# The second half of a batch's value products moved into the next round, and its inverses behind the next statistics

## The chip, the cores and the metric

The kernel runs on one core of a Trainium2 chip. The metric is the device time of one execution in microseconds (us). In the profile PE is the matrix engine (TensorE; PEld are its weight loads), DVE the vector engine, ACT the scalar engine, POOL the GpSimd engine, and SP the engine that issues most DMAs. L939 is line 939 of the kernel before.

## The reference

One transformer block over a batch of 32, each with 165 tokens (a class token, 36 image patches, 128 text tokens) of width 256. The change touches the attention alone.

```python
h = tok_ref(x)                               # 1 + 36 embedded patches per batch
h = concatenate([h, txt], axis=1)            # (32, 165, 256)
h = h + attn(layernorm(h))                   # 16 heads of 16, causal mask, every 4th key dropped
h = h + ffn(layernorm(h))                    # router, 8 experts, the top 660 tokens of each

def attn(x):
    q, k, v = heads(x @ Wq + bq), heads(x @ Wk + bk), heads(x @ Wv + bv)
    att = einsum('bhtd,bhsd->bhts', q, k) / sqrt(16)
    att = softmax(where(mask == 0, -inf, att), axis=-1)
    return (einsum('bhts,bhsd->bhtd', att, v)) @ Wp + bp
```

## The kernel before

Each engine has its own program, written out by hand in a fixed order, and the programs meet at semaphores. The attention part is a software pipeline of rounds, `for b in ROUNDS`: round b works at several batches at once. In round b the matrix engine makes the queries, keys and values of batch b+2, the masked scores by rows of batch b+1 (`row_scores`, from which the vector engine takes the row maxima), and the scores by keys of batch b (`key_scores`), their exponentials being the probabilities. Batches go in pairs n = b // 2, u = b % 2: an even round also projects the pair before and adds the result to the residual, an odd round also transposes and routes the pair before that.

What the change touches:

- `mix_values(b, c)` on the matrix engine (L939): the value products of heads 8c to 8c+7 of batch b, and beside them the row sums of the probabilities by products with ones, into bank 2+c. It is made of four groups (V, ones, V, ones) of four products, each 32 columns of weights wide, side by side in the array. It waits for `causal_done`: GpSimd has put zeros where a key is later than the query (`zero_future`, L535, once for each quarter of the heads). Half c = 1 needs the last two of the four quarters.
- `heads_out(b, c)` on the vector engine: waits for `pv_done`, takes the inverse of the row sums (L1309) and multiplies the products by it (L1313), into `yT`.
- `queries(b + 2)` (L862) stands at the head of a round on the matrix engine; in a round after an odd one `route` (L965, ends the round before) stands ahead of it, and `copy_logits` (L1319) takes its result.
- `ln1_stats_of` (even rounds) and `ln2_stats_of` (odd rounds) on the vector engine: `bn_stats` (L1246) and `bn_aggr` (L1250), ahead of the round's row maxima.
- `row_max(m, i)`, i = 0 to 4 (L1298), with `low_q` and `low_k` (L1277) between. `row_scores(m, i)` (L898 for the mask, L901 for the products) alternates between banks 4 and 5: number i waits until the maxima of number i-2 are taken. `row_scores(m, 4)` (the form 65*65 of L898) so waits for `row_max(m, 2)`.
- SP packs the queries and keys (`pack`, L364 and L368) once `low_q` is done (`q_ready`), and behind that, in its own order, the maxima (`pack_max`, L373), which the next round's first `key_scores` needs (`m_packed`).

Of the kernel before, what the change touches and what calls it, by code (L numbers as in the profile page):

```python
# [15 lines left out]
B, CH, IMG, PATCH = 32, 3, 96, 16  # L16
# [110 lines left out]
def build(nc, xT, wl, h0, addrows, clsrows, minus, watt, vecs, rowv, w1, w2, const_f, const_b, out):  # L127
    ctx = ExitStack()
    with ctx:  # L129
# [135 lines left out]
        def bank(i):  # L265
            return ps_all[:, i, :]
# [57 lines left out]
        def apart(eng):  # L324

            eng.sem_inc(passed[eng], 1)
# [506 lines left out]
        def _(pe):  # L833
# [22 lines left out]
            def queries(n, free):  # L856
                u, h = n % 2, n // 2 % 2
                pe.wait_ge(xnT_ready, 2 * (n // 2) + 2)
                pe.wait_ge(*free)
                for c in range(KD):  # L860
                    for k in range(KD):
                        mm = pe.matmul(bank(6)[:, c * TE:(c + 1) * TE], W_q[:, k, c * 128:(c + 1) * 128],  # L862
                                       xnT[:, h, k, u * T:u * T + TE], start=(k == 0), stop=(k == KD - 1))
                mm.then_inc(q_done, 1)
# [63 lines left out]
            def mix_values(b, c):  # L928
                pe.wait_ge(causal_done, 4 * b + 2 * c + 2)
                if c == 0:  # L930
                    pe.wait_ge(v_ready, b + 1)
                if b >= 1:
                    pe.wait_ge(yT_ready, 2 * b + c - 1)
                for w in range(2):
                    for part in range(2):
                        for j in range(4):
                            dst = bank(2 + c)[32 * j:32 * j + 32, part * T:(part + 1) * T]
                            lhs = v_rows(b % 3, w, 4 * c + j)[0:S] if part == 0 else ones_eo[0:S, w, :]
                            mm = pe.matmul(dst, lhs, PT[0:S, 2 * c + w, j, :], start=(w == 0 and part == 0),  # L939
                                           stop=(w == 1), skip_group_check=True)  # L940
                mm.then_inc(pv_done, 1)
# [27 lines left out]
            def query_bank(b):  # L969
                n, u = divmod(b, 2)  # L970
                if b == -2:
                    return xnT_ready, 2
                if u == 1:
                    return (resid_ready, RT * (n - 1) + 2) if n >= 1 else (v_ready, b + 2)
                return (xn2T_ready, 2 * (n - 2) + 2) if n >= 2 else (xnT_ready, 2 * (n + 1) + 2)
# [46 lines left out]
            def round_of(b):  # L1022
                n, u = divmod(b, 2)
                has_q, has_r, has_s = b + 2 < B, b + 1 < B, b < B
                has_t1, has_p, m = n + 2 < NPAIR, 0 <= n - 1 < NPAIR, b + 1
                if has_q:
                    queries(b + 2, query_bank(b))
                if has_s:
                    key_scores(b, 0)
                if has_r:  # L1030
                    row_scores(m, 0, (max_ready, 5 * m))
                if has_q:
                    keys(b + 2, key_bank(b))
                if has_r:
                    row_scores(m, 1, (mT_ready, m))
                if has_s:
                    key_scores(b, 1)
                if has_r:
                    row_scores(m, 2, (max_ready, 5 * m + 1))
                if has_q:  # L1040
                    values(b + 2)
                if has_r:
                    row_scores(m, 3, (max_ready, 5 * m + 2))
                if has_r:
                    row_scores(m, 4, (max_ready, 5 * m + 3))
                if has_s:
                    key_scores(b, 2)
                if b == B:
                    project(n - 1, 0, (exp_done, 4 * B))
                    project(n - 1, 1, (exp_done, 4 * B))  # L1050
                    project(n - 1, 2, (max_ready, 5 * B))
                    route(n - 2)
                    return
                if u == 0 and has_p:
                    project(n - 1, 0, (k_ready, b + 3) if has_q else (logit_ready, n - 1))
                if u == 1 and has_t1:
                    transposes1(n + 2, 0, (k_ready, b + 3))
                if has_r:
                    max_transposes(m)
                if u == 0 and has_p:  # L1060
                    project(n - 1, 1, (v_ready, b + 3) if has_q else (xn2T_ready, 2 * (n - 2) + 2))
                if u == 1 and has_t1:
                    transposes1(n + 2, 1, (v_ready, b + 3))
                if has_s:
                    key_scores(b, 3)
                if u == 0 and has_p:
                    project(n - 1, 2, (resid_ready, RT * (n - 1) + 1))
                if b == B - 1:
                    mix_values(b, 0)
                    mix_values(b, 1)  # L1070
                if u == 1 and has_p:
                    for c in range(KD):
                        transposes2(n - 1, c, (xnT_ready, 2 * (n + 2) + c + 1) if has_t1 else
                                    ((k_ready, v_ready)[c], b + 3) if has_q else
                                    (resid_ready, RT * (n - 1) + 3 - c) if has_s else
                                    ((logit_ready, n - 1), (xn2T_ready, 2 * (n - 1)))[c])
                if has_s and b != B - 1:
                    mix_values(b, 0)
                    mix_values(b, 1)
                if u == 1 and has_p and b != B - 1:  # L1080
                    route(n - 1)

# [148 lines left out]
        def _(dve):  # L1231
# [29 lines left out]
            def ln2_stats_of(p):  # L1261
                dve.wait_ge(resid_ready, RT * p + RT)
                apart(dve)
                if p >= 1:
                    dve.wait_ge(shift2_ready, p)
                stats(p, st2, mv2, ln2_chain, ln2_stats)
# [56 lines left out]
            def round_of(b):  # L1323
                n, u = divmod(b, 2)
                has_q, has_r, has_s, has_p = -2 <= b < B - 2, -1 <= b < B - 1, 0 <= b < B, 0 <= n - 1 < NPAIR
                if b == -4:
                    embedded(1)
                if b == -2:
                    low_q(0)
                    low_k(0)  # L1330
                if u == 0 and n + 2 < NPAIR:
                    ln1_stats_of(n + 2)
                if u == 1 and has_p:
                    ln2_stats_of(n - 1)
                if b == B + 1:
                    copy_logits(n - 2)
                if b == -4:
                    for g in (2, 3, 4, 5):
                        embedded(g)
                if b == -3:  # L1340
                    dve.wait_ge(vec_in, 16)
                    for k in range(KD):
                        ins = dve.tensor_copy(bvB[:, k, :], bvT[:, k:k + 1].to_broadcast([128, A]))
                    ins.then_inc(bvB_ready, 1)
                    embedded(6)
                if b == -1:
                    for g in (7, 8):
                        embedded(g)
                    low_q(1)
                    low_k(1)  # L1350
                    embedded(9)
                    dve.wait_ge(bpe_done, 1)
                    dve.wait_ge(row_in, 16)
                    dve.tensor_tensor(bpe[0:A, :], bank(5)[0:A, 0:D], bp_s[0:A, :], ALU.add).then_inc(bpe_ready, 1)
                    embedded(10)
                if has_r:
                    row_max(b + 1, 0)
                if has_q and b >= 0:
                    low_q(b + 2)
                if has_r:  # L1360
                    row_max(b + 1, 1)
                if has_q and b >= 0:
                    low_k(b + 2)
                if has_r:
                    row_max(b + 1, 2)
                if has_r:
                    row_max(b + 1, 3)
                if has_r:
                    row_max(b + 1, 4)
                    copy_mT(b + 1)  # L1370
                if u == 0 and has_p:
                    for r in range(RT):
                        residual(n - 1, r)
                if has_s:
                    heads_out(b, 0)
                    heads_out(b, 1)
                if u == 1 and has_p and b != B - 1:
                    copy_logits(n - 1)

            embedded(0)  # L1380
            for b in ROUNDS:
                round_of(b)
# [350 lines left out]
```

## Time and profile before

| | |
|---|---|
| median of 3 runs | 832.5 us (829.48 to 835.09) |
| the profiled execution's own time | 832.7 us |
| its span in the trace | 831.0 us |
| PE busy | 739.2 us, 89% of the span |
| DVE, ACT, POOL busy | 68%, 48%, 46% |
| granted clock of TensorE, mean | 0.938 |
| attention rounds in the trace | about 50 to 455 us |

How to read it: a row of the timeline gives the start, the duration and the engine of a run of like instructions, and in brackets the time that the engine sat idle before it and what ended that. The rounds repeat: from round 3 on, two rounds take 25.5 us, and rows of one pair of rounds stand for the others. Rows below are of rounds 12 (even, from 204.12 us on the matrix engine) and 13 (from 216.34 us).

### The profile page before, as it was taken

Reading aid. Unit: us, or ns where it says so; the run is one execution under the profiler, and the core shown is the slowest. Engines: PE = TensorE matmul, PEld = TensorE weight load, DVE = VectorE, ACT = ScalarE, POOL = GpSimd, SP = SyncE. Lnnn points to the kernel's source line nnn. Section 1 sums busy time; section 2 is a strip of 40 time slices with the busy share of each in tenths; the row PEclk is TensorE's granted clock in tenths of the full one; section 3 lists DMA queues with packets and bytes.
Section 4 is the critical chain, followed back from the end, with each engine's and each line's share of the span. In section 5 each row is a group of like instructions: output and inputs, shape, how many; then the busy total and the mean of one; then the engine's idle time right before and its main releaser. Section 6 shows DMA issues by size and latency. Waiting matters only on the chain. (4 is left out here: it accounts for less than half of the span.)

```text
span 831.0 us, 18782 instructions
## 1 busy us (share of the span) xinstructions
PE 739.2 (89%) x6840; PEld 670.2 (81%) x6840; DVE 566.7 (68%) x1343; ACT 397.2 (48%) x858; POOL 384.1 (46%) x534
## 2 busy tenths in 40 slices
PE   6989999999999999999997412499999999999994
PEld 4878888888888888888875311399999999999994
DVE  1357778677686776776765377857788787787461
ACT  0334464454544554545543264045737558376470
POOL 4243464554544645546434342304735637356334
PEclk9999999999999999999998655569999999999998
DMA  9765766866747756568560522102345343443122
GB/s 311 202 100 93 112 111 110 141 109 113 108 94 113 117 93 88 106 100 122 97 101 20 185 77 95 33 1 84 59 127 148 42 135 59 124 100 40 33 29 33
DMA packets 80584, 82.38 MB, mean 99 GB/s; under 512 B 35705, under 2 KB 73575, under 8 KB 80236
## 3 DMA queue, kind: packets, MB, share of 16 engines
q1 hardware_dynamic: 66988, 64.96, 39.4%
q0 software_dynamic: 11840, 11.12, 8.3%
q10 hardware_dynamic: 1664, 5.09, 2.0%
q8 instruction: 55, 0.90, 0.5%
q14 instruction: 37, 0.30, 0.1%
HBM read 34.59 MB, written 16.22 MB: 61 GB/s over the span
## 5 line engine op out<-in xcount | busy, mean ns | idle before, releaser
L631 POOL DMA_INDIRECT out<-r_arena x48 | 81.3, 1695 | 116.3 <-DVE r_arena L1594 104.4
L535 POOL TENSOR_SCALAR_AFFINE_SELECT r_arena<-r_arena 126x660 f32<-126x660 f32 x128 | 97.0, 768 | 51.6 <-ACT r_arena L695 51.3
L695 ACT ACTIVATE r_arena<-ps_all 126x660 f32<-126x660 f32 x128 | 92.2, 720 | 57.5 <-PE ps_all L924 56.2
L1298 DVE TENSOR_REDUCE mx<-ps_all 128x4 f32<-128x504 f32 (+1 forms) x160 | 104.8, 668 | 15.8 <-PE ps_all L901 14.5
L1309 DVE RECIPROCAL r_arena<-ps_all 128x165 f32<-128x165 f32 x64 | 76.1, 1189 | 57.3 <-PE ps_all L939 57.3
L1616 DVE TENSOR_TENSOR hT_lo<-r_arena,hT_hi 128x330 fp32r<-128x330 f32 x128 | 63.3, 501 | 40.7 <-ACT r_arena L803 40.7
L901 PE MATMUL ps_all<-Kp,Qp 96*65 96x56 f32 (+1 forms) x512 | 90.6, 293 | 0.0
L618 POOL DMA_INDIRECT xe<-xn_rows,r_arena x48 | 60.3, 1255 | 62.4 <-issue 35.7
L924 PE MATMUL ps_all<-Qp,Kp 98*126 98x166 f32 x512 | 84.6, 288 | 4.5 <-ACT r_arena L695 2.9
L801 ACT ACTIVATE hT_hi<-ps_all,vec_s 128x330 fp32r<-128x330 f32 x128 | 68.9, 538 | 38.2 <-PE ps_all L1166 37.3
L1166 PE MATMUL ps_all<-xeT_hi,W_hi 128*128 128x330 f32 x256 | 83.5, 326 | 1.1 <-DVE xeT_lo L1608 1.1
L1166 PE MATMUL ps_all<-xeT_lo,W_hi 128*128 128x330 f32 x256 | 82.6, 323 | 0.0
L1166 PE MATMUL ps_all<-xeT_hi,W_lo 128*128 128x330 f32 x256 | 82.2, 321 | 0.0
L1186 PE MATMUL ps_all<-hT_hi,W_hi 128*128 128x330 f32 x256 | 81.6, 319 | 0.0
L1186 PE MATMUL ps_all<-hT_hi,W_lo 128*128 128x330 f32 x256 | 80.7, 315 | 0.0
L673 ACT ACTIVATE q_hi<-ps_all,vec_s 128x166 fp32r<-128x166 f32 x64 | 22.0, 395 | 122.2 <-PE ps_all L862 122.2
L1186 PE MATMUL ps_all<-hT_lo,W_hi 128*128 128x330 f32 x256 | 80.3, 314 | 0.0
L924 PEld LDWEIGHTS ps_all<-Qp,Kp 98*126 98x126 f32 x512 | 69.0, 190 | 10.1 <-ACT r_arena L695 6.5
L901 PEld LDWEIGHTS ps_all<-Kp,Qp 96*65 96x65 f32 (+1 forms) x512 | 66.8, 166 | 5.6
L803 ACT ACTIVATE r_arena<-ps_all,vec_s 128x330 f32<-128x330 f32 x128 | 67.9, 530 | 0.0
L939 PE MATMUL ps_all<-r_arena,V 126*32 126x165 f32 x1024 | 61.6, 313 | 1.1 <-POOL r_arena L535 1.0
L939 PE MATMUL ps_all<-r_arena,cf 126*32 126x165 f32 x1024 | 60.5, 309 | 0.0
(182 smaller groups left out, 1699.5 us busy)
## 6 DMA issues: line engine op xcount, KB each, us to landing
H<-w SPq DMA_DIRECT2D x16, 1024.0 KB, 5.8
Qp<-q_hi SPq DMA_DIRECT2D x64, 166.0 KB, 3.9
Kp<-k_hi SPq DMA_DIRECT2D x128, 63.0 KB, 4.0
Qp<-q_lo SPq DMA_DIRECT2D x32, 166.0 KB, 4.6
out<-H SPq DMA_DIRECT2D x16, 330.0 KB
xn_rows<-r_arena SPq DMA_DIRECT2D x16, 330.0 KB
Kp<-k_lo SPq DMA_DIRECT2D x64, 63.0 KB, 4.0
H<-h SPq DMA_DIRECT2D x11, 336.0 KB, 3.9
```

Source lines behind the costliest of these rows:

```text
L535: pool.affine_select(PT[0:S, g, :, :], PT[0:S, g, :, :], [[0, 4], [STEP - 1, T]], ALU.is_ge, 0.0, base=STEP - 2, channel_multiplier=-STEP) ...
L631: pool.indirect_dma_start(rows_out, bass.IndirectOffsetOnAxis(tok[0:A, e % NTB, a:a + 1], 0), yw[0:A, a, :], None, bounds_check=NTOK - 1, ...
L695: act.activation(PT[0:S, g, :, :].rearrange("p (k h) t -> p k h t", k=2), pair[:, :, :, 0:T], ACT.Exp, scale=float(HD) ** -0.5).then_inc(e ...
L801: act.activation(hT_hi[:, f, j * HALF:(j + 1) * HALF], bank(n % 4)[:, 0:HALF], ACT.Gelu, bias=b1_s[:, e, f:f + 1]).then_inc(gelu_done, 1)
L803: act.activation(h_raw[:, n % 4, :], bank(n % 4)[:, 0:HALF], ACT.Gelu, bias=b1_s[:, e, f:f + 1]).then_inc(gelu_done, 1)
L901: mm = pe.matmul(dst[0:rows, 2 * j * cols:2 * (j + 1) * cols].rearrange("p (w s) -> p w s", w=2), Qp[0:MROW, q, h, at_row:at_row + rows], ...
L924: mm = pe.matmul(dst[0:S, j * TE:(j + 1) * TE], Kp[0:MROW + 2, q, h, g % 2, :], Qp[0:MROW + 2, q, h, :], start=(j == 0), stop=(j == 1), sk ...
L939: mm = pe.matmul(dst, lhs, PT[0:S, 2 * c + w, j, :], start=(w == 0 and part == 0), stop=(w == 1), skip_group_check=True)
L1166: mm = pe.matmul(bank(n % 4)[:, 0:HALF], w[:, k, f * 128:(f + 1) * 128], x[:, k, cols], start=(i == 0), stop=(i == len(terms) - 1))
L1186: mm = pe.matmul(bank(4 + c)[:, 0:HALF], w[:, f, c * 128:(c + 1) * 128], h[:, f, cols], start=(i == 0), stop=(i == len(terms) - 1))
L1298: dve.tensor_reduce(dst, src, AX.X, ALU.max).then_inc(max_ready, 1)
L1309: dve.reciprocal(rS[:, c, :], bank(2 + c)[:, T:2 * T]).then_inc(rs_sum, 1)
```

## The change

On the matrix engine `mix_values(b, 1)` leaves the end of round b and stands in round b+1 behind `queries(b + 3)` and ahead of that round's first `key_scores`. On the vector engine `heads_out(b, 1)` leaves the end of round b and stands in round b+1 behind the statistics and ahead of the first `row_max`. The last batch keeps its order. No instruction is added or removed, and the other engines' programs stay as they are.

```diff
@@ tensor engine, round_of(b)
                 if has_q:
                     queries(b + 2, query_bank(b))
+                if 1 <= b < B:
+                    mix_values(b - 1, 1)
                 if has_s:
                     key_scores(b, 0)
...
                 if has_s and b != B - 1:
                     mix_values(b, 0)
-                    mix_values(b, 1)
                 if u == 1 and has_p and b != B - 1:
                     route(n - 1)
@@ vector engine, round_of(b)
                 if u == 1 and has_p:
                     ln2_stats_of(n - 1)
+                if 1 <= b < B:
+                    heads_out(b - 1, 1)
...
                 if has_s:
                     heads_out(b, 0)
+                if b == B - 1:
                     heads_out(b, 1)
                 if u == 1 and has_p and b != B - 1:
                     copy_logits(n - 1)
```

The matrix engine before, from an odd round's end into the even one; `V` holds the values, `cf` the ones, `r_arena` the probabilities, L965 is the routing, L862 the queries, L924 the first scores by keys:

```order
L939 MATMUL ps_all<-r_arena,V 32x165 x4
L939 MATMUL ps_all<-r_arena,cf 32x165 x4
L939 MATMUL ps_all<-r_arena,V 32x165 x4
L939 MATMUL ps_all<-r_arena,cf 32x165 x4
L939 MATMUL ps_all<-r_arena,V 32x165 x4
L939 MATMUL ps_all<-r_arena,cf 32x165 x4
L939 MATMUL ps_all<-r_arena,V 32x165 x4
L939 MATMUL ps_all<-r_arena,cf 32x165 x4
L965 MATMUL ps_all<-vec_s,r_arena 110x8 x6
L862 MATMUL ps_all<-xnT,W_s 128x166 x4
L924 MATMUL ps_all<-Qp,Kp 126x166 x4
```

The same place on the matrix engine now:

```order
L939 MATMUL ps_all<-r_arena,V 32x165 x4
L939 MATMUL ps_all<-r_arena,cf 32x165 x4
L939 MATMUL ps_all<-r_arena,V 32x165 x4
L939 MATMUL ps_all<-r_arena,cf 32x165 x4
L965 MATMUL ps_all<-vec_s,r_arena 110x8 x6
L862 MATMUL ps_all<-xnT,W_s 128x166 x4
L939 MATMUL ps_all<-r_arena,V 32x165 x4
L939 MATMUL ps_all<-r_arena,cf 32x165 x4
L939 MATMUL ps_all<-r_arena,V 32x165 x4
L939 MATMUL ps_all<-r_arena,cf 32x165 x4
L924 MATMUL ps_all<-Qp,Kp 126x166 x4
```

The second half of the value products went behind the routing and the queries; from an even round into an odd one it is the same without L965.

The vector engine before, at the same seam from an odd round into an even one:

```order
L1304 CAST mT<-ps_all 16x165
L1309 RECIPROCAL r_arena<-ps_all 128x165
L1313 TENSOR_TENSOR r_arena<-ps_all,r_arena 128x165
L1309 RECIPROCAL r_arena<-ps_all 128x165
L1313 TENSOR_TENSOR r_arena<-ps_all,r_arena 128x165
L1319 TENSOR_TENSOR L<-ps_all,row_s 110x24
L1246 BN_STATS st<-H 110x6 x3
L1250 BN_AGGR mv<-st 110x2 x3
L1298 TENSOR_REDUCE mx<-ps_all 128x2x2
```

The vector engine there now (the changed file has these lines one further down):

```order
L1305 CAST mT<-ps_all 16x165
L1310 RECIPROCAL r_arena<-ps_all 128x165
L1314 TENSOR_TENSOR r_arena<-ps_all,r_arena 128x165
L1320 TENSOR_TENSOR L<-ps_all,row_s 110x24
L1247 BN_STATS st<-H 110x6 x3
L1251 BN_AGGR mv<-st 110x2 x3
L1310 RECIPROCAL r_arena<-ps_all 128x165
L1314 TENSOR_TENSOR r_arena<-ps_all,r_arena 128x165
L1299 TENSOR_REDUCE mx<-ps_all 128x2x2
```

The second inverse and its product went behind the logits and the statistics, and stand directly ahead of the first row maximum.

## Rows read from the trace of the kernel before

**Rows 1.** The page: span, busy time, granted clock in 40 slices

```profile
span 831.0 us, 18782 instructions
PE 739.2 (89%) x6840; PEld 670.2 (81%) x6840; DVE 566.7 (68%) x1343; ACT 397.2 (48%) x858; POOL 384.1 (46%) x534
PEclk9999999999999999999998655569999999999998
```

**Rows 2.** Timeline of PE, end of round 11 and head of round 12

```profile
200.44 0.49 PE L939 MATMUL ps_all<-r_arena,V 126*32 126x165 f32 x8
201.69 0.49 PE L939 MATMUL ps_all<-r_arena,V 126*32 126x165 f32 x8
202.27 0.46 PE L939 MATMUL ps_all<-r_arena,V 126*32 126x165 f32 x8
202.55 0.46 PE L939 MATMUL ps_all<-r_arena,cf 126*32 126x165 f32 x8
...
202.94 0.46 PE L965 MATMUL ps_all<-vec_s,r_arena 128*110 128x8 f32 x3
...
204.12 1.37 PE L862 MATMUL ps_all<-xnT,W_s 128*128 128x166 f32 x8
205.22 0.68 PE L924 MATMUL ps_all<-Qp,Kp 98*126 98x166 f32 x4
...
209.54 0.35 PE L898 MATMUL ps_all<-cb 65*65 65x448 bf16 x1
```

**Rows 3.** Timelines of PEld and ACT at the same seam

```profile
201.68 0.16 PEld L939 LDWEIGHTS ps_all<-r_arena,V 126*32 126x32 f32 x8 [0.24 <-POOL r_arena L535]
...
200.59 0.78 ACT L704 ACTIVATE r_arena<-ps_all 128x330 f32<-128x330 f32 x2
```

**Rows 4.** Line L939 by itself: what ended PE's idle time before it (us, times)

```profile
  POOL r_arena L535: 6.3, 18
```

**Rows 5.** Timeline of DVE, head of round 12

```profile
201.84 1.20 DVE L1309 RECIPROCAL r_arena<-ps_all 128x165 f32<-128x165 f32 x1 [2.47 <-PE ps_all L939]
...
206.36 0.68 DVE L1298 TENSOR_REDUCE mx<-ps_all 128x4 f32<-128x504 f32 x1
```

**Rows 6.** Timeline of DVE, end of round 12 and head of round 13

```profile
215.36 1.20 DVE L1309 RECIPROCAL r_arena<-ps_all 128x165 f32<-128x165 f32 x1 [0.86 <-PE ps_all L939]
...
216.83 1.18 DVE L1309 RECIPROCAL r_arena<-ps_all 128x165 f32<-128x165 f32 x1
...
218.29 1.07 DVE L1246 BATCH_NORM_STATS2 st<-H 110x6 f32<-110x256 f32 x3
...
219.62 0.68 DVE L1298 TENSOR_REDUCE mx<-ps_all 128x4 f32<-128x504 f32 x1
```

**Rows 7.** Timelines of PEld and PE, round 13

```profile
213.96 0.16 PEld L939 LDWEIGHTS ps_all<-r_arena,V 126*32 126x32 f32 x8 [0.35 <-issue]
...
217.46 0.69 PE L924 MATMUL ps_all<-Qp,Kp 98*126 98x166 f32 x4
...
220.36 0.10 PEld L898 LDWEIGHTS ps_all<-cb 128*128 128x128 bf16 x1 [0.26 <-DVE mx L1298]
...
220.95 0.73 PEld L881 LDWEIGHTS ps_all<-W_s,xnK 128*126 128x126 f32 x4 [0.22 <-DVE q_lo L1277]
...
222.64 0.11 PEld L898 LDWEIGHTS ps_all<-cb 65*65 65x65 bf16 x1 [0.36 <-DVE mx L1298]
```

**Rows 8.** Timeline of SP's issues, and PE waiting for such a DMA

```profile
62.65 0.67 SPq L373 DMA_DIRECT2D Qp<-mT  x1
...
214.32 0.69 SPq L373 DMA_DIRECT2D Qp<-mT  x1
...
65.94 0.68 PE L924 MATMUL ps_all<-Qp,Kp 98*126 98x166 f32 x4 [0.19 <-DMA Qp<-mT]
```

**Rows 9.** Timeline of DVE, head of round 2

```profile
74.34 1.20 DVE L1309 RECIPROCAL r_arena<-ps_all 128x165 f32<-128x165 f32 x1 [1.89 <-PE ps_all L939]
...
78.95 0.68 DVE L1298 TENSOR_REDUCE mx<-ps_all 128x4 f32<-128x504 f32 x1
```

## The prediction

> **What bounds the kernel now.** I read the page first: 831.0 us of span, PE busy for 89% of it, and the granted clock at nine tenths or more all through the first 22 slices, so the attention rounds run at the upper level, 2.4 GHz [rows 1]. The profiled execution took 832.7 us, the median is 832.5 us; my sum is made on 832.7, which is 1.7 us over the span and 0.2 us over the median. Nothing outside the rounds is touched. Then I read PE's timeline over two rounds, 12 and 13, and DVE's beside it. An even round's start to the next even round's takes 25.5 us. PE sits idle only in slivers, so the question is which sliver goes and which comes.
>
> The wait that the change aims at is the one for the last zeros under the mask: in an odd round the second half of the value products starts 1.25 us after the first [rows 2], with 0.24 us of idle weight load ahead of it, ended by POOL [rows 3]. Without a wait the four groups take 1.14 us (three gaps of 0.28, as from 202.27 to 202.55 [rows 2], and 0.30 for the first), so the wait costs 0.1 us in an odd round, and in an even one nothing. Over the whole run POOL held this line for 6.3 us in 18 cases [rows 4]; most of that is weight load idle that the product before covers.
>
> The other thing to see is how DVE stands at the head of a round. In the odd round 13 it is busy without a break from the first inverse at 215.36 us to the first row maximum at 219.62: inverse and product, inverse and product, statistics [rows 6]. That is late: PE stands still for it three times, 0.26, 0.22 and 0.36 us, the last at 222.64 [rows 7]. So from the end of the first half of the value products to 222.64 an odd round is set by DVE, and 222.64 is 3.02 us after the row maximum's start. In the even round 12 the first row maximum starts at 206.36 [rows 5] and PE's fifth set of row scores at 209.54 without any wait [rows 2]. That is 3.18 us, so the even round has 0.16 us to spare against DVE's 3.02.
>
> **The change part by part.**
>
> *The wait for the zeros* goes: behind the first half stands the routing (odd into even) or the queries, over 1 us of work. The routing needs ACT's copies, which end at 201.37 [rows 3], before the first half's end near 201.58. Gain 0.1 us in each even round's head.
>
> *Seams on PE.* The value products use 32 columns of weights at a time, the others up to 128. Leaving them costs something: the last group starts at 202.55 and the next kind of product at 202.94, 0.39 us against 0.28 between groups [rows 2], so 0.11 us. Entering has no clean row: the weight load is idle for 0.35 us before the first group [rows 7], which bounds it from above, and nothing bounds it from below but zero; I take 0.1, as on leaving. Before there was one way in and one out per round, now there are two: 0.2 us more per round, between 0.1 and 0.46.
>
> The Trainium skill (TensorEngine Tiling (Array Packing), section Tiling Modes) says that changing the tiling mode drains the engine. By that rule each moved half pays a whole drain twice, where my sum takes 0.2 us; the 0.39 us against 0.28 agrees that something is paid, and is far from a whole idle stretch. The rival below on the seams has its price.
>
> *Even rounds, PE alone.* From the first half at 200.44: routing at 201.69 (1.25 us, as the second half's 201.69 to 202.94 with its seam), queries 1.18 us later at 202.87, second half 1.10 + 0.10 later at 204.07, first key scores 1.25 later at 205.32, against 205.22 now [rows 2]. So PE alone loses 0.1 us.
>
> *Even rounds, DVE.* An inverse starts 1.40 us after its half does (200.44 to 201.84 [rows 2, 5]). The second half now starts at 204.07, so its inverse starts at 205.47. Until then DVE does the first inverse with its product (1.47 us, 215.36 to 216.83), copies the logits (under 0.1) and makes the statistics (1.33 us, 218.29 to 219.62) [rows 6], is done by about 204.9, and **waits half a microsecond**. Then inverse and product, 1.46 us, and the first row maximum starts at 206.93 instead of 206.36: 0.57 late. The spare 0.16 us takes a part, and PE's fifth set of row scores starts at 206.93 + 3.02 = 209.95 instead of 209.54. That is **0.41 us lost in each even round**; the 0.1 us of PE alone lies inside it. What comes behind is PE's work back to back, so the loss stays. The rounds with a routing ahead are 4, 6 to 28, thirteen: 13 x 0.41 = 5.3 us. (Round 28 has no statistics, but there too the inverse waits for PE until 205.47 in these times.)
>
> *Odd rounds.* Here no routing stands between, so the second half starts 1.25 + 1.10 + 0.1 - 0.02 = about 2.43 us after the first at 213.96 and its inverse could start 1.40 us later, at 217.79. DVE comes there only at 216.83 + 1.33 = 218.16. It does not wait, does the same work in another order, and starts the row maximum at 219.62 as before. PE, 0.2 us late from its seams, meets its three stops (0.84 us in sum) a bit later and is held by the last of them as now. Cost 0. The cover is DVE's lateness; if it were gone, 0.2 us in each of 14 rounds, 2.8 us.
>
> *Statistics come 1.5 us earlier*, and with them POOL's and ACT's part of the layer norm. I find no place where PE waits for those in these rounds: worth 0.
>
> *SP.* It stays in its order: the packing waits for `low_q`, which follows the first row maximum and is 0.57 us later in even rounds, and the maxima's DMA at 214.32 stands behind nine others. It would go out at 214.89. The one wait for it that shows took 3.29 us from issue to PE's start (62.65 to 65.94), so it lands by 218.2 [rows 8]. The odd round's key scores come at 217.46 [rows 7] + 0.41 + 0.2 = 218.07. At most 0.1 us is lost, inside the odd round's 0.84 us of stops. Cost 0, but close.
>
> *Start and end.* In round 2 DVE is late too (first row maximum at 78.95 [rows 9]), and there it waited for the zeros between its two inverses. Now: 74.34 + 1.47 + 1.33 + 1.46 = 78.60, a gain of 0.35 us. In round 1 the key scores wait for the maxima's DMA [rows 8] whatever stands ahead, so nothing comes of its shorter wait. Round 30 loses its 0.1 to 0.2 us of seam.
>
> **Sum:** + 5.3 - 0.35 + 0.15 = + 5.1 us on 832.7, so **837.9 us**. With the seams at their lower bound the even round's inverse comes 0.1 us earlier, 13 x 0.31 - 0.3 = + 3.7 us (836.4); with the upper bound below, 841.
>
> **The rivals.**
>
> *The late row maximum does not reach PE.* The 0.16 us of spare rests on one pair of rounds and on the 3.02 us being the same in both; if DVE makes up its 0.57 us (its row maxima have idle time between them in even rounds), only PE's own 0.1 us is left, 13 x 0.1 - 0.35 = + 1 us, 833.7; with seams at zero, 13 x -0.1 - 0.35, about 831. For it: even rounds have no DVE wait of PE at all before. Against: the odd rounds show the same chain, fully packed, holding PE.
>
> *The seams cost all that is idle before them* (0.46 us a round instead of 0.2). Even rounds: the second half and its inverse come 0.25 us later, 0.66 us lost, 13 x 0.66 = 8.6 and + 8.4 in all, 841.1. Odd rounds still hide it. (A drain at each change, as the Trainium skill has it on its page TensorEngine Tiling (Array Packing), section Tiling Modes, would give this case.)
>
> *Slower: the maxima's DMA becomes what odd rounds wait for.* If it takes so long behind the later packing that the key scores start over 0.84 - 0.2 = 0.6 us late, the stops no longer hide it. Each 0.5 us beyond costs 14 x 0.5 = 7 us: 845. It decides from a landing 0.6 us later than I reckon, against 3.29 us at the most in the row. This is the case that ends clearly slower.
>
> *Faster.* The odd rounds' three stops go, because the head of the DVE chain is untied from the second half: 14 x 0.84 = 11.8 us gained, 821 to 826 with what even rounds lose. Against it: DVE was busy throughout that stretch and gets no less work, so its row maximum cannot come earlier.
>
> **How the numbers follow.** Forecast 837.9 (836 to 840.5): 0.55. Late maximum absorbed, 831 to 834.5: 0.2. Seams dear, 840.5 to 842: 0.12. DMA, about 845: 0.07. Faster, 821 to 826: 0.06. The range 831.0 to 842.5 leaves out the last two. A difference under 1% (8.3 us) is about what runs of this kernel can't tell from none. Below 824.2: 0.06; above 840.8: 0.15; between: 0.79.
>
> **What the changed profile would show.** POOL no longer ends idle time before the value products from round 3 on. In even rounds DVE is idle about 0.5 us before the second inverse, ended by PE's value products; the first row maximum starts 6.5 us after the first half instead of 5.9; and PE is idle before the 65*65 form of L898's line, ended by DVE, in even rounds too. Two rounds take 25.9 us instead of 25.5. I am wrong if two rounds take 25.5 or less (the chain was absorbed), or if PE's first key scores of an odd round have a DMA behind their idle time and the odd round has grown. Seams are read as the start of the key scores less the start of the second half (1.25), and less the queries ahead.

## The result, and the profile after

The changed kernel takes 839.0 us (median of 7 runs, 835.93 to 841.75) against 832.5 us before (7 runs), a ratio of 1.0078 with a 95% interval of 1.0057 to 1.0100: slower by 6.5 us. The forecast was 837.9 us. The profiled execution after took 837.54 us with a span of 835.8 us.

Two rounds can be timed by the start of the first transpose of the row maxima (L908), which stands once in each round. The timeline of PE before, rounds 11, 12 and 13:

```profile
198.68 0.23 PE L908 MATMUL ps_all<-cf,mx 65*16 65x65 f32 x1
...
211.54 0.22 PE L908 MATMUL ps_all<-cf,mx 65*16 65x65 f32 x1
...
224.18 0.22 PE L908 MATMUL ps_all<-cf,mx 65*16 65x65 f32 x1
```

And after:

```profile
200.39 0.23 PE L908 MATMUL ps_all<-cf,mx 65*16 65x65 f32 x1
...
213.81 0.22 PE L908 MATMUL ps_all<-cf,mx 65*16 65x65 f32 x1
...
226.41 0.23 PE L908 MATMUL ps_all<-cf,mx 65*16 65x65 f32 x1
```

The way into an even round's transposes went from 12.86 to 13.42 us, into an odd round's from 12.64 to 12.60. Below "even" and "odd" are these two lengths (12.87 and 12.64 in most pairs before), and all of the loss sits in the even ones. Thirteen of them (rounds 4 to 28) at 0.55 us less 0.04 for each odd one are 6.6 us. In the two traces the rounds 4 to 29 differ by 6.3 us, because round 18 of the execution before took 0.29 us more than its neighbours (13.16 us).

The end of round 11 and round 12 on PE after, where the second half now follows the routing and the queries (to set beside [rows 2]):

```profile
202.16 0.49 PE L939 MATMUL ps_all<-r_arena,V 126*32 126x165 f32 x8
...
203.41 1.33 PE L965 MATMUL ps_all<-vec_s,r_arena 128*110 128x8 f32 x12
204.60 1.37 PE L862 MATMUL ps_all<-xnT,W_s 128*128 128x166 f32 x8
205.90 0.49 PE L939 MATMUL ps_all<-r_arena,V 126*32 126x165 f32 x8
...
207.16 0.67 PE L924 MATMUL ps_all<-Qp,Kp 98*126 98x166 f32 x4
...
211.78 0.38 PE L898 MATMUL ps_all<-cb 65*65 65x448 bf16 x1 [0.16 <-DVE mx L1299]
```

The same stretch on DVE (to set beside [rows 5]):

```profile
203.55 1.20 DVE L1310 RECIPROCAL r_arena<-ps_all 128x165 f32<-128x165 f32 x1 [2.47 <-PE ps_all L939]
204.78 0.33 DVE L1314 TENSOR_TENSOR r_arena<-ps_all,r_arena 128x165 f32<-128x165 f32 x1
205.03 0.17 DVE L1320 TENSOR_TENSOR L<-ps_all,row_s 110x24 f32<-110x24 f32 x1
205.12 1.07 DVE L1247 BATCH_NORM_STATS2 st<-H 110x6 f32<-110x256 f32 x3
206.10 0.41 DVE L1251 BATCH_NORM_AGGREGATE mv<-st 110x2 f32<-110x6 f32 x3
207.29 1.19 DVE L1310 RECIPROCAL r_arena<-ps_all 128x165 f32<-128x165 f32 x1 [0.78 <-PE ps_all L939]
208.52 0.33 DVE L1314 TENSOR_TENSOR r_arena<-ps_all,r_arena 128x165 f32<-128x165 f32 x1
208.77 0.67 DVE L1299 TENSOR_REDUCE mx<-ps_all 128x4 f32<-128x504 f32 x1
```

Read both together, from the first half's start at 202.16. DVE has done the statistics at 206.5 and then waits 0.78 us for the second half, which PE began at 205.90. Its first row maximum starts 6.61 us after the first half (5.92 before), and PE's fifth set of row scores (the form 65*65 of L898) 9.62 us after it (9.10 before), now with DVE named as what ended its idle time. From the row maximum to that set it is 3.01 us, as the 3.02 of the odd round before.

Round 13 after, DVE and then PE's weight loads (to set beside [rows 6, 7]):

```profile
217.63 1.20 DVE L1310 RECIPROCAL r_arena<-ps_all 128x165 f32<-128x165 f32 x1 [0.86 <-PE ps_all L939]
...
219.10 1.07 DVE L1247 BATCH_NORM_STATS2 st<-H 110x6 f32<-110x256 f32 x3
...
220.42 1.16 DVE L1310 RECIPROCAL r_arena<-ps_all 128x165 f32<-128x165 f32 x1
...
221.86 0.67 DVE L1299 TENSOR_REDUCE mx<-ps_all 128x4 f32<-128x504 f32 x1
```

```profile
218.82 0.16 PEld L939 LDWEIGHTS ps_all<-r_arena,V 126*32 126x32 f32 x8 [0.18 <-issue]
...
222.70 0.10 PEld L898 LDWEIGHTS ps_all<-cb 128*128 128x128 bf16 x1
...
224.88 0.11 PEld L898 LDWEIGHTS ps_all<-cb 65*65 65x65 bf16 x1 [0.36 <-DVE mx L1299]
```

DVE does not wait for the second half here. 4.23 us after its first inverse it is at the row maximum (4.26 before), and the last of PE's three stops is as before; the first two are gone, because PE itself comes later.

The span grew by 4.8 us, less than what the rounds lost. The last group of the attention's value products starts at 453.94 us before and at 461.57 after, 7.6 us later. Some 1.3 to 1.5 us of that is a stretch at the lower clock level (1.2 GHz) on the way from round 29 into round 30 (window, its length, busy times of PE, PEld, DVE, ACT and POOL, and granted clock, DMA share and GB/s as the last three), after:

```profile
436.00:440.00 4.00, 4.00 (x46) 2.75 (x44) 0.75 (x1) 1.30 (x3) 0.81 (x2) 0.59 0.48 91
```

The same piece of the program, some 6 us earlier in the execution before (430 to 434 us), has a granted clock of 1.00.

About 2.8 us came back at the first expert, where the clock rose sooner after the sparse stretch of the routing search: the expert's first product starts 7.6 us later than before (545.22 against 537.59), the last one ahead of its next pause 4.8 us later (558.49 against 553.68). The windows of that piece, shifted by the 7.6 us, after:

```profile
542.00:558.00 16.00, 14.14 (x104) 13.80 (x105) 13.51 (x28) 7.13 (x16) 2.58 (x3) 0.69 0.08 24
```

and before:

```profile
534.40:550.40 16.00, 14.17 (x86) 13.79 (x87) 10.62 (x25) 4.47 (x11) 2.55 (x3) 0.50 0.09 25
```

These belong to the two executions; the medians, 6.5 us apart, show what the rounds lost.

### The profile page after: what moved, and what is told of

It is laid out like the page before. It is cut to its first block and busy times, and to the rows that moved or that the text cites. A ratio compares the mean times of both kernels' runs of the same rounds, so it can differ in the third digit from the quotient of the medians.

```text
span 835.8 us, 18782 instructions
## 1 busy us (share of the span) xinstructions
PE 744.8 (89%) x6840; PEld 667.4 (80%) x6840; DVE 564.8 (68%) x1343; ACT 398.7 (48%) x858; POOL 387.8 (46%) x534
## 5 line engine op out<-in xcount | busy, mean ns | idle before, releaser
L901 PE MATMUL ps_all<-Kp,Qp 96*65 96x56 f32 (+1 forms) x512 | 92.3, 292 | 0.0
L924 PE MATMUL ps_all<-Qp,Kp 98*126 98x166 f32 x512 | 84.3, 288 | 5.2 <-ACT r_arena L695 2.9
L924 PEld LDWEIGHTS ps_all<-Qp,Kp 98*126 98x126 f32 x512 | 68.0, 190 | 18.3 <-issue 7.5
L939 PE MATMUL ps_all<-r_arena,V 126*32 126x165 f32 x1024 | 62.6, 317 | 0.0
L939 PE MATMUL ps_all<-r_arena,cf 126*32 126x165 f32 x1024 | 61.1, 311 | 0.0
```

Source lines behind the costliest of these rows:

```text
L901: mm = pe.matmul(dst[0:rows, 2 * j * cols:2 * (j + 1) * cols].rearrange("p (w s) -> p w s", w=2), Qp[0:MROW, q, h, at_row:at_row + rows], ...
L924: mm = pe.matmul(dst[0:S, j * TE:(j + 1) * TE], Kp[0:MROW + 2, q, h, g % 2, :], Qp[0:MROW + 2, q, h, :], start=(j == 0), stop=(j == 1), sk ...
```

## The experiments

Ratios are to the kernel before on the same chip, whose median there was 833.7 to 834.2 us instead of 832.5 (the changed kernel's ratio is to the 832.5). The first two medians are of 7 runs. The others are of 10, but the move into even rounds, PE's move alone and the last row have 4, and the late inverse has 6. All lengths are from the start of L908 to the next, as above.

| kernel | median us | ratio, 95% interval | even | odd |
|---|---|---|---|---|
| before | 832.5 | | 12.87 | 12.64 |
| changed | 839.0 | 1.0078 (1.0057 to 1.0100) | 13.42 | 12.60 |
| moved into odd rounds only | 832.84 | 0.9987 (0.9962 to 1.0012) | 12.88 | 12.59 |
| moved into even rounds only | 842.3 | 1.0091 (1.0056 to 1.0127) | 13.42 | 12.64 |
| second half ahead of the queries | 833.75 | 1.0003 (0.9969 to 1.0038) | 12.98 | 12.59 |
| inverse of one column | 835.9 | 1.0018 (0.9988 to 1.0048) | 13.08 | 12.59 |
| DVE's move alone | 838.96 | 1.0066 (1.0039 to 1.0093) | 13.54 | 12.60 |
| DVE's move, logits too | 832.57 | 0.9983 (0.9958 to 1.0008) | 12.87 | 12.60 |
| PE's move alone | 875.68 | 1.0485 (1.0436 to 1.0534) | 14.85 | 13.75 |
| before, late inverse in odd rounds | 820.1 | 0.9826 (0.9782 to 0.9871) | 12.87 | 11.75 |
| the same, second half moved into odd rounds | 826.21 | 0.9898 (0.9862 to 0.9934) | 12.87 | 12.08 |

My theory is that of the prediction: in even rounds DVE's second inverse waits for PE's displaced second half, and through the row maxima PE waits for DVE. The rival is that the seams of the narrow products on PE are the cost, wherever they stand.

**The move into one kind of round only.** In the tensor engine's and the vector engine's program alike (here for odd rounds; for even ones with `u == 0`):

```diff
-                if 1 <= b < B:
+                if 1 <= b < B and u == 1:
                     mix_values(b - 1, 1)
...
                     mix_values(b, 0)
+                    if u == 1:
+                        mix_values(b, 1)
```

> The second half of the value products and its inverse move as in the change, but only from an even round into an odd one; into even rounds all is as before. My theory (odd rounds are held by the vector engine, which takes the same work in another order): two rounds stay at 25.5 us, and the time is that of before, 831 to 834 us, although each odd round has both extra seams on PE. The rival (what the change costs is the seams of the narrow products on PE, wherever they are): 15 odd rounds at 0.3 us, 837 us or more.

> The counterpart: the move only from an odd round into an even one. My theory: all of the loss is here, two rounds take 26.0 us as in the changed kernel, 838 to 840 us. The rival (seams alone): half of the loss, 835 to 836 us.

Measured: into odd rounds only, nothing is lost (ratio 0.9987, its interval holds 1), though the extra seams of those rounds are all there (the rival's 837 us would be a ratio of 1.003, outside the interval); into even rounds only, the even length is 13.42 us as in the changed kernel and the time 842.3 us. The whole loss is in the even rounds. The 842.3 missed the 838 to 840 expected. The kernel before stood at 834.17 beside it, and the ratio's interval holds the changed kernel's 1.0078; the lengths account for 7 of the 8 us, and the rest, in four runs, stays open.

**The second half ahead of the queries.**

```diff
+                if 1 <= b < B:
+                    mix_values(b - 1, 1)
                 if has_q:
                     queries(b + 2, query_bank(b))
-                if 1 <= b < B:
-                    mix_values(b - 1, 1)
```

> As the change, but on PE the second half stands ahead of the next round's queries; into an even round it is still behind the routing. The vector engine's order is that of the change. In even rounds the second half now ends 1.2 us earlier, before the vector engine is done with the statistics. My theory (the loss is the vector engine's wait for the second half): the first row maximum of an even round starts as early as before, two rounds take 25.5 to 25.7 us, 832 to 835 us. The rival (seams alone, and the same two extra seams stand in even rounds): 26.0 us for two rounds in the end, 838 us.

The timeline of DVE in round 12:

```profile
204.46 0.41 DVE L1251 BATCH_NORM_AGGREGATE mv<-st 110x2 f32<-110x6 f32 x3
204.79 1.16 DVE L1310 RECIPROCAL r_arena<-ps_all 128x165 f32<-128x165 f32 x1
...
206.54 0.69 DVE L1299 TENSOR_REDUCE mx<-ps_all 128x4 f32<-128x504 f32 x1 [0.23 <-PE ps_all L901]
```

The inverse follows the statistics without a wait, and the row maximum waits for PE again, not PE for it. The even length is 12.98: of 0.55 us, 0.11 are left. Two rounds take 25.57 us, as expected.

Not all of the 0.44 us that came back is DVE's wait. PE enters the second half from the routing here:

```profile
201.77 1.32 PE L965 MATMUL ps_all<-vec_s,r_arena 128*110 128x8 f32 x12
203.03 0.49 PE L939 MATMUL ps_all<-r_arena,V 126*32 126x165 f32 x8
```

That is 1.26 us from start to start, against 1.18 from the routing to the queries before (202.94 to 204.12 [rows 2]): this entry costs 0.08 us, where the entry from the queries costs 0.21 (below). So 0.13 us of the 0.44 are a cheaper seam, and about 0.31 are left for DVE.

**An inverse of one column.** PE's order is that of the change, DVE has 1.0 us less to do behind its wait (0.20 us from the inverse to its product, instead of 1.23).

```diff
-                dve.reciprocal(rS[:, c, :], bank(2 + c)[:, T:2 * T]).then_inc(rs_sum, 1)
+                w = 1 if c == 1 and u == 1 and b < B - 1 else T
+                dve.reciprocal(rS[:, c, 0:w], bank(2 + c)[:, T:T + w]).then_inc(rs_sum, 1)
```

> The changed kernel, but the second half of odd batches takes its inverse of one column only instead of 165 and multiplies by old inverses, so this part of the output is wrong; the last batch is left whole. That takes 1.1 us from the vector engine between its wait for the second half and the first row maximum in even rounds; PE's work and its seams stay. My theory: even rounds are then PE's own, 0.2 us longer than before by the seams, two rounds take 25.7 us, 834 to 836 us. The rival (seams alone): no difference from the changed kernel, 26.0 us.

DVE in round 12:

```profile
205.30 0.17 DVE L1311 RECIPROCAL r_arena<-ps_all 128x1 f32<-128x1 f32 x1 [0.78 <-PE ps_all L939]
205.50 0.33 DVE L1315 TENSOR_TENSOR r_arena<-ps_all,r_arena 128x165 f32<-128x165 f32 x1
206.28 0.68 DVE L1299 TENSOR_REDUCE mx<-ps_all 128x4 f32<-128x504 f32 x1 [0.46 <-PE ps_all L901]
```

The wait for the second half is the same 0.78 us, but now DVE is in time for the row scores. The even length is 13.08, so 0.34 of the 0.55 us go through DVE's chain; 0.21 is what PE's own order costs there. The changed kernel's trace has the same figure: from the first half to the first key scores PE takes 5.00 us (202.16 to 207.16) against 4.78 before (200.44 to 205.22 [rows 2]). Two rounds take 25.67 us, as expected; the rival's 26.0 did not come.

**DVE's half of the change alone.** The second inverse behind the statistics as in the change's diff, PE as before.

> The vector engine's half of the change alone: the second inverse behind the statistics, PE as before. My theory: the second half is long done when the vector engine comes to it, no wait arises, the order of equal work changes nothing, two rounds 25.5 us, 831 to 834 us. A rival (the order on the vector engine itself costs, by pushing the inverse against the maxima): slower than 836 us.

This expectation missed: 838.96 us, an even length of 13.54. I had not looked at what else the shorter head of the chain would meet: DVE in round 12,

```profile
205.12 0.33 DVE L1313 TENSOR_TENSOR r_arena<-ps_all,r_arena 128x165 f32<-128x165 f32 x1
206.37 0.18 DVE L1319 TENSOR_TENSOR L<-ps_all,row_s 110x24 f32<-110x24 f32 x1 [0.91 <-PE ps_all L965]
...
209.22 0.67 DVE L1298 TENSOR_REDUCE mx<-ps_all 128x4 f32<-128x504 f32 x1
```

The logits came up 1.5 us earlier, ahead of the routing's end, and the statistics, inverse and row maxima queued behind that wait. In the changed kernel the routing comes earlier too, so this wait is absent there. (In round 28, which has no statistics, the even length was 12.87.) To see that it was the wait and not the order, the logits went behind the statistics as well:

```diff
+                if u == 0 and 4 <= b < B:
+                    copy_logits(n - 2)
                 if 1 <= b < B:
                     heads_out(b - 1, 1)
...
-                if u == 1 and has_p and b != B - 1:
+                if b == B + 1:
                     copy_logits(n - 1)
```

> The vector engine's half of the change alone, as before, but the logits are copied behind the statistics too. In the run without this the logits came ahead of the statistics and right behind the first product, and waited 0.91 us for PE's routing, which stands behind both halves there; each even round lost 0.67 us. If that wait was the cause, two rounds take 25.5 us again and the time is that of before, 832 to 835 us. If the order of inverse and statistics itself costs, two rounds stay at 26.1 us, 838 us or more.

Measured 832.57 us, even length 12.87: the order by itself costs nothing.

**PE's half of the change alone.** The second half behind the queries, DVE's inverse ahead of the statistics as before.

> PE's half of the change alone: the second half behind the queries, the vector engine as before, with the second inverse ahead of the statistics. My theory: it waits for the second half and the statistics stand behind that wait, so the first row maximum is 1.4 us later than in the changed kernel in even rounds and 1.1 us in odd ones; two rounds take about 28.4 us and the time is 870 us or so. If only the seams counted it would be as the changed kernel, 838 us.

Two rounds take 28.60 us and the time is 875.68 us, near the 28.4 and 870 expected. The change's DVE part is thus what keeps most of the price of its PE part away.

**The inverse where DVE has time.** In odd rounds the kernel before is held by DVE's late row maxima. One move takes an inverse and its product out of that stretch (the kernel before, DVE alone):

```diff
+                if has_s and u == 1:
+                    heads_out(b - 1, 1)
                 if has_s:
                     heads_out(b, 0)
+                if has_s and u == 1:
                     heads_out(b, 1)
```

> The kernel before, with one move on the vector engine alone: the second inverse and product of an even batch stand behind the next (odd) round's five row maxima and their copy instead of ahead of its statistics. Nobody needs them earlier than the end of that round, and 2.5 us are idle there. My theory (odd rounds are held by the vector engine's late start on the row maxima): PE's three stops of 0.84 us go, 14 rounds give 8 to 11 us, 822 to 825 us, two rounds take 24.7 to 24.9 us. The rival (PE's own work bounds odd rounds too, the stops are covered elsewhere): no difference from 832.5 us.

DVE from the end of round 12 to the next even one:

```profile
210.45 1.20 DVE L1309 RECIPROCAL r_arena<-ps_all 128x165 f32<-128x165 f32 x1 [0.87 <-PE ps_all L939]
...
211.93 1.07 DVE L1246 BATCH_NORM_STATS2 st<-H 110x6 f32<-110x256 f32 x3
...
213.69 0.69 DVE L1298 TENSOR_REDUCE mx<-ps_all 128x4 f32<-128x504 f32 x1 [0.37 <-PE ps_all L901]
...
219.00 1.17 DVE L1309 RECIPROCAL r_arena<-ps_all 128x165 f32<-128x165 f32 x1
...
221.54 1.19 DVE L1309 RECIPROCAL r_arena<-ps_all 128x165 f32<-128x165 f32 x1 [1.00 <-PE ps_all L939]
```

The row maximum waits 0.37 us for PE instead of the other way round, the displaced inverse at 219.00 fits in before the next one's 1.00 us of idle time, and the odd length falls from 12.64 to 11.75 us. 820.1 us: 14 rounds at 0.89 are 12.5 us of the 14.1 that lie between it and the 834.2 of the kernel before beside it. That is 1.7% (interval 1.3 to 2.2%) below the kernel before and, by the two ratios, 2.5% below the changed one. The expectation took the right cause and too small a gain: 24.62 us for two rounds lie under its 24.7 to 24.9, and 820.1 under its 822 to 825. The three stops are 0.84 us together, and the odd length fell by 0.89.

**The seams without cover.** In that version odd rounds are PE's own. The second half moved behind the queries in odd rounds alone then shows the seams:

> The second half moves behind the queries into odd rounds only, and the vector engine takes its inverse behind that round's row maxima, so that odd rounds are no longer held by the vector engine: PE's two extra seams stand there without cover. Against the same kernel with the second half left in place (odd rounds of 11.75 us) this shows what the seams cost. My theory, from the starts in the changed kernel (routing, queries and second half take 5.00 us there against 4.78, with a wait of 0.1 us gone): 12.0 to 12.1 us per odd round, 14 x 0.3 = 4 us more, 823 to 826 us. If the seams cost nothing of their own: 11.75 and 820 us; if a whole drain of 0.6 us: 12.35 and 828 us or more.

PE at the head of round 13 with the move:

```profile
214.17 1.40 PE L862 MATMUL ps_all<-xnT,W_s 128*128 128x166 f32 x8
215.50 0.49 PE L939 MATMUL ps_all<-r_arena,V 126*32 126x165 f32 x8
...
216.36 0.46 PE L939 MATMUL ps_all<-r_arena,cf 126*32 126x165 f32 x8
216.76 0.67 PE L924 MATMUL ps_all<-Qp,Kp 98*126 98x166 f32 x4
```

and without it:

```profile
211.43 1.40 PE L862 MATMUL ps_all<-xnT,W_s 128*128 128x166 f32 x8
212.55 0.69 PE L924 MATMUL ps_all<-Qp,Kp 98*126 98x166 f32 x4
```

The queries take 1.33 us to the next start ahead of the narrow products and 1.12 ahead of the key scores: entering costs 0.21 us. Leaving costs 0.40 - 0.28 = 0.12 (216.36 to 216.76, less the step between groups). Together 0.33, and the odd length grew by 0.33 (11.75 to 12.08), less than the 12.35 of the larger rival. The medians of the two versions, taken on two chips, are 6.1 us apart; 14 x 0.33 = 4.6 are these seams, and the rest is not explained (four and six runs). The 826.21 is just over the 823 to 826 expected.

## Why the prediction was right

The time, 839.0 against 837.9 us, and the way there held. Two rounds take 26.02 us, against 25.9. Part of the closeness is luck: the main term was a fifth too small, the odd rounds gave back 0.5 us that I had not counted, and the interval of the ratio allows 4.7 to 8.3 us. My remark that runs of this kernel can't tell a difference under 1% from none was too cautious; seven runs of each told 0.8% apart.

- **The wait for the zeros** was worth 0.1 us in an even round's head, as costed. It went: in the trace after, no idle time ahead of the value products is ended by POOL. No more came of it.
- **Seams:** predicted 0.2 us a round (0.1 for entering), measured 0.33. Leaving was right at 0.12; entering is 0.21, a little over half of my upper bound of 0.35. The rival on the seams, at 0.46 a round, was too dear by as much as my 0.2 was too cheap. The Trainium skill (TensorEngine Tiling (Array Packing), Tiling Modes) says that a change of tiling mode drains the engine. By that rule, the trace agrees that each passage costs, at 0.08 to 0.21 us; whether it is a drain that takes this time, no run here shows.
- **Even rounds, DVE:** predicted a wait of about half a microsecond, a row maximum 0.57 us later and 0.41 us lost. Measured 0.78, 0.69 and 0.52 (0.55 over the whole even round). The term was too small by the 0.11 us of the dearer seam. The statistics' end was also added up wrong: 201.84 + 1.47 + 0.1 + 1.33 is 204.74, not 204.9, so by my own terms the wait was 0.73 us; nothing behind it used that number. That the loss goes through DVE is shown by the inverse of one column (0.34 us back) and, less the cheaper seam, by the second half ahead of the queries (about 0.31 back). With DVE in time PE alone lost 0.21 us, where I had 0.1.
- **Odd rounds, cost 0 under DVE's lateness:** shown by the move into odd rounds alone (0.9987). They even became 0.04 us shorter, as did DVE's way from the first inverse to the row maximum (4.23 us instead of 4.26); DVE's new order is enough for that (12.60 with DVE's move alone). The cover was thinner than I had it: in round 13 the second half starts 2.59 us after the first, not 2.43, and its inverse could have started 0.2 us before DVE came to it (220.22 against 220.42), where I had 0.37. The price without the cover, 0.2 us predicted, is 0.33.
- **SP and the maxima's DMA, cost 0:** no such wait shows in the steady odd rounds, and these did not grow. It was close: in round 13 the maxima's DMA goes out at 216.74 and PE's key scores start at 220.08, 3.34 us later. In round 1 PE waited for it 0.78 us instead of 0.19, and in round 2 for 0.30 us where it had not waited before. The kernel before had three such waits, not the one that I named; none of the three was longer than 3.29 us from issue to start.
- **Round 2** gained 0.39 us (12.25 to 11.86), against 0.35.
- **Sum:** predicted 5.1 us; the steady rounds gave 6.6, less 0.4 in round 2, against 6.5 between the medians.
- **The clock:** the page has nine tenths or more in the first 21 slices, not 22. The 22nd (about 436 to 457 us) reads 8; the last value products lie in it. The steady rounds are not touched by this.
- **The rivals:** the late row maximum did reach PE, in all thirteen even rounds. "Faster" failed for the reason given, DVE got no less work; the late inverse, which does take work from that stretch, gained 12.5 us in the odd rounds, against the 11.8 I had priced for their stops.

## What to carry to other kernels

A half of a step that is moved later on one engine can become a wait on the next. Before hiding a 0.1 us wait behind other work, look at who stands behind the moved step's consumer and how much spare time they have (here 0.16 us). Where an engine comes late to the step that others wait for, look for work ahead of it that nobody needs yet and for its own idle time in the same round; moving one inverse there gave 1.7%. And when a step is taken away from the head of a queue, read what comes up behind it: the logits' wait of 0.91 us had been invisible behind the inverse.

## What was new about the hardware

Going from the 128-wide queries into the 32-wide value products costs PE 0.21 us (from the routing, 0.08) and coming out 0.12 us, also when the profile shows nothing that PE waits for: the weight loads then have 0.18 and 0.26 us of idle time, put down to `issue`. So the idle time of the weight loads overstates the cost on the way out.

The clock fell to 1.2 GHz on the way into round 30 in the profiled execution after (0.59 over 436 to 440 us, with PE busy for 3.36 of the 4 us before), and not in the one before. The way into round 30's transposes took 12.83 us instead of 11.13; with the inverse of one column, which has the same order on PE, the clock stayed at 1.00 there and it took 11.49. With the 2.8 us at the first expert, where the two executions rose to 2.4 GHz at different points of the program, single executions of this kernel can't be compared to better than a few us. Whether the change had a part in where the clock fell was not tried. PE's new order isn't needed for it: with DVE's move alone, PE's order being that of before, the clock fell in the same place (0.77 and 0.81 over 440 to 448 us). And 25 runs of the kernel before, taken beside the first experiments, range from 829.9 to 839.94 us, at mean granted clocks of 0.940 and 0.927.
